# Turning the rank stacks on VectorE in squares of 32, in a kernel of four chained adapter layers

## What is computed

```python
x = x + _L0_cond_ref(...)  # x @ W.T + 2 * gated expert adapters of rank 16, top 2 of 8
x = x + _L1_cond_ref(...)  # W = weights[condition]; einsum('bct,bcd->bdt', x, W)
x = x + _L2_cond_ref(...)  # Bx = einsum('bni,bri->bnr', x, B[ids]); einsum('bnr,bor->bno', Bx, A[ids])
x = x + _L3_cond_ref(...)  # x @ W.T + b + ((x @ A[ids]) @ Bm[ids]) * 2, rank 16
```

## Time and profile before

| | us |
|---|---|
| median of three runs | 906.36 (905.24 to 906.5) |
| the profiled execution | 905.11 |
| its span, first to last instruction | 903.3 |
| TensorE busy | 894.3 |
| VectorE busy | 557.0 |
| ScalarE busy | 346.6 |
| GpSimd busy | 235.9 |

### The profile page before, as it was taken

The page is one execution under the profiler, slowest core; times in us unless marked ns, Lnnn a source line. Parts: engine busy times, 40 slices in busy tenths (PEclk is TensorE's granted clock), DMA queues, the critical chain, the costliest instruction groups (busy, mean ns, idle before and its releaser), DMA issues.

```text
span 903.3 us, 14862 instructions
## 1 busy us (share of the span) xinstructions
PE 894.3 (99%) x4758; PEld 794.6 (88%) x4758; DVE 557.0 (62%) x1421; ACT 346.6 (38%) x800; POOL 235.9 (26%) x379
## 2 busy tenths in 40 slices
PE   8999999999999999999999999999999999999997
PEld 7888888888888888998998998998999999999997
DVE  6554444444367526567667677677676686686675
ACT  5543343333334332333433434424434334334333
POOL 1010010011010003524424425415415325235240
PEclk9999999999999999999999999999999999999999
DMA  7878686999663564666765766666567567667665
GB/s 251 306 249 292 209 255 204 311 337 266 186 193 124 167 197 143 179 181 188 214 183 179 209 198 192 194 199 210 172 202 221 174 181 221 185 183 218 186 197 155
DMA packets 105602, 187.69 MB, mean 208 GB/s; under 512 B 15926, under 2 KB 66870, under 8 KB 105526
## 3 DMA queue, kind: packets, MB, share of 16 engines
q1 hardware_dynamic: 105526, 186.76, 67.6%
HBM read 143.20 MB, written 49.81 MB: 214 GB/s over the span
## 4 chain that ended last, share of the span: by engine, by line
PE 91%; SPq 3%; DMA 2%; issue 1%; POOL 1%; DVE 0%; ACT 0%; DVEq 0%; POOLq 0%
PE ps_o L1407 27%; PE ps_d L1433 17%; PE ps_w L1441 13%; PE ps_d L1441 10%; PE ps_s L1407 8%; PE ps_o L1454 5%; PE ps_d L1448 4%; PE ps_o L1465 2%; DMA mdraw<-t 1%; PE ps_s L1471 1%; SPq L445 1%; PE ps_w L1448 1%; DMA stat_raw<-stat 1%; SPq L403 1%; PE ps_o L1503 0%
## 5 line engine op out<-in xcount | busy, mean ns | idle before, releaser
L1042 DVE TENSOR_TENSOR stat_lo<-stat_raw,stat_hi 128x1024 fp32r<-128x1024 f32 (+1 forms) x127 | 147.5, 1162 | 26.5 <-ACT stat_hi L773 24.2
L773 ACT ACTIVATE stat_hi<-stat_raw 128x1024 fp32r<-128x1024 f32 (+1 forms) x127 | 116.9, 933 | 22.3 <-POOL stat_raw L657 7.5
L1433 PE MATMUL ps_d<-w_hi,stat_hi 128*128 128x512 f32 x256 | 104.9, 410 | 0.7 <-POOL w_lo L682 0.7
L1433 PE MATMUL ps_d<-w_lo,stat_hi 128*128 128x512 f32 x256 | 101.2, 395 | 0.0
L1433 PE MATMUL ps_d<-w_hi,stat_lo 128*128 128x512 f32 x256 | 100.8, 394 | 0.0
L1407 PE MATMUL ps_o<-chunk_a_hi,stat_hi 128*128 128x512 f32 x216 | 84.4, 391 | 0.9 <-DVE stat_lo L1042 0.9
L1407 PE MATMUL ps_o<-chunk_a_hi,stat_lo 128*128 128x512 f32 x216 | 84.1, 389 | 0.0
L1407 PE MATMUL ps_o<-chunk_a_lo,stat_hi 128*128 128x512 f32 x216 | 84.0, 389 | 0.0
L682 POOL CAST w_hi<-mdraw 128x512 fp32r<-128x512 f32 x32 | 19.6, 613 | 206.1 <-DMA mdraw<-t 206.1
L657 POOL TENSOR_TENSOR stat_raw<-stat_raw,ident 128x128 f32<-128x128 f32 x40 | 22.9, 574 | 184.2 <-DMA stat_raw<-stat 184.2
L1407 PE MATMUL ps_o<-chunk_b_hi,stat_hi 128*128 128x512 f32 x152 | 59.1, 389 | 0.0
(11 more groups left out here) (226 smaller groups left out, 2266.7 us busy)
## 6 DMA issues: line engine op xcount, KB each, us to landing
up<-tu SPq DMA_DIRECT2D x124, 256.0 KB, 4.3
stat_raw<-stat SPq DMA_DIRECT2D x59, 512.0 KB, 4.4
mdraw<-t SPq DMA_DIRECT2D x128, 208.0 KB, 2.9
stat_raw<-x SPq DMA_DIRECT2D x32, 512.0 KB, 3.5
out<-outb SPq DMA_DIRECT2D x30, 512.0 KB, 5.3
t<-md_a SPq DMA_DIRECT2D x16, 576.0 KB, 5.8
rows_raw<-x SPq DMA_DIRECT2D x32, 256.0 KB, 3.4
chunk_a_raw<-mov SPq DMA_DIRECT2D x24, 256.0 KB, 5.1
```

What stands on the lines that cost most here:

```text
L773: return nc.scalar.activation(dst, src, ACT.Copy)
L1042: return nc.vector.tensor_tensor(out=dst, in0=src, in1=rounded.bitcast(F32), op=ALU.subtract)
L1433: last = nc.tensor.matmul(plain_bank(t)[:, 0:WCOLS], rows[a][:, k, :], w[c][:, k, :], start=k == 0 and m == 0, stop=k == KB - 1 and m == l ...
```

## The change

The transpositions on TensorE (`h2_rows`, `h3_rows`) go. After each stack VectorE writes the transposed stack to a tile `turned` in SBUF, in eight squares of 32x32 (`turn_ranks`), and ScalarE rounds `turned` into `h2T` or `h3T`. The stacks are 64 columns wide instead of 128, both batch rows in the same columns; the zero blocks are in `turned`, cleared once. There is one `turned`, so a turn waits until the copy of the turn ahead has been made; since `h2T` is now overwritten without a step of TensorE in between, its copy waits until the products of the tile ahead are done. In the last pair some steps of `ranks` are written in another order. The number that a turn has in the order is given by `h2_place` and `h3_place`.

```diff
-        h2stack = sb("h2stack", [P, BT, RANK, 2, 2], F32R)
-        h3stack = sb("h3stack", [P, BT, RANK, 2, 2], F32R)
+        h2stack = sb("h2stack", [P, RANK, 2, 2], F32R)
+        h3stack = sb("h3stack", [P, RANK, 2, 2], F32R)
+        turned = sb("turned", [P, TOKENS])
...
+        def h2_place(turn):
+            return 2 * turn + (0 if at(turn, TURN_A) else 1)
+        def h3_place(turn):
+            return 2 * turn + (3 if at(turn, TURN_B) else 2)
...
             def h2_hi(t):
                 act.wait_ge(pe_h, t + 1)
+                if not at(t, 0):
+                    act.wait_ge(dve_turned, h2_place(t - 1))
...
             def h2T_copy(t):
-                act.wait_ge(pe_h2T, t + 1)
-                round_to(h2T[:, :], ps_h2T).then_inc(act_h2T, 1)
+                act.wait_ge(dve_turned, h2_place(t))
+                if not at(t, 0):
+                    act.wait_ge(pe_up2, t)
+                    act.wait_ge(pe_h3, t)
+                round_to(h2T[:, :], turned[:, :]).then_inc(act_turned, 1)
...
             def h3T_copy(t):
-                act.wait_ge(pe_h3T, t + 1)
-                round_to(h3T[:, :], ps_h3T).then_inc(act_h3T, 1)
+                act.wait_ge(dve_turned, h3_place(t))
+                if not at(t, 0):
+                    act.wait_ge(pe_out[2], t)
+                round_to(h3T[:, :], turned[:, :]).then_inc(act_turned, 1)
...
+            def turn_ranks(stacked, place):
+                flat = stacked[:, :, :, :].rearrange("p r h e -> p (r h e)").bitcast(F32)
+                if place > 1:
+                    dve.wait_ge(act_turned, place - 1)
+                for b in range(BT):
+                    for i in range(b * TB, (b + 1) * TB, SQUARE):
+                        for q in range(0, 4 * RANK, SQUARE):
+                            row = b * 4 * RANK + q
+                            last = nc.vector.transpose(turned[row:row + SQUARE, i:i + SQUARE],
+                                                       flat[i:i + SQUARE, q:q + SQUARE])
+                last.then_inc(dve_turned, 1)
...
                 last.then_inc(dve_h2, 1)
+                dve.wait_ge(dve_h2, t + 1)
+                turn_ranks(h2stack, h2_place(t))
...
             def ranks2(t):
-                pe.wait_ge(act_h2T, t + 1)
+                pe.wait_ge(act_turned, h2_place(t))
...
-                plain(a, range(0, 3))
-                if fin:
-                    h3_rows(b2)
-                plain(a, range(3, 5))
+                plain(a, range(0, 5))
                 if fin:
                     ranks3(b2)
...
                 winograd(ps_w, A11, B11, True).then_inc(pe_p[0], 1)
-                if back:
-                    pe.wait_ge(dve_vsum, 2 * a + 2)
-                    pe.wait_ge(dve_h2, a1 + 1)
-                    h2_rows(a1)
...
-                plain(b, range(0, HALF_KB))
+                plain(b, range(KB)).then_inc(pe_hl, 1)
+                if back:
+                    ranks3(a1)
                 pe.wait_ge(dve_udb, a + 1)
-                if back:
-                    h3_rows(a1)
-                plain(b, range(HALF_KB, KB)).then_inc(pe_hl, 1)
-                if back:
-                    ranks3(a1)
                 gated_rows(a)
```

More of the change, by code:

```diff
@@ L361, in build @@
         pe_out = [sem(f"pe_out{n}") for n in range(3)]
-        CONSTS = 6
+        CONSTS = 5
+        SQUARE = 32
         SETS = BT + 8
@@ L893, in h2_hi @@
                 act.wait_ge(pe_h, t + 1)
+                if not at(t, 0):
+                    act.wait_ge(dve_turned, h2_place(t - 1))
                 for b in range(BT):
                     rows = slice(b * TB, (b + 1) * TB)
-                    last = round_to(h2stack[rows, b, :, :, 0], hidden(t, rows, slice(b * RANK, (b + 1) * RANK)))
+                    last = round_to(h2stack[rows, :, :, 0], hidden(t, rows, slice(b * RANK, (b + 1) * RANK)))
                 last.then_inc(act_h2, 1)
@@ L900, in h3_hi @@
                 act.wait_ge(pe_h3, t + 1)
+                if not at(t, 0):
+                    act.wait_ge(dve_turned, h3_place(t - 1))
                 for b in range(BT):
                     rows = slice(b * TB, (b + 1) * TB)
-                    last = nc.scalar.activation(h3stack[rows, b, :, :, 0], hidden(t, rows, slice(BR + b * RANK, BR + (b + 1) * RANK)),
+                    last = nc.scalar.activation(h3stack[rows, :, :, 0], hidden(t, rows, slice(BR + b * RANK, BR + (b + 1) * RANK)),
                                                 ACT.Copy, scale=SCALE3)
@@ L1210, in mix_lo, with stack_lo @@
                 rest(mix[t % 2][lo][:, :], mixid[t % 2][:, :], mix[t % 2][hi][:, :]).then_inc(dve_mix, 1)
-            def stack_lo(t, rows, b, cols, stacked, scale):
+            def stack_lo(t, rows, cols, stacked, scale):
                 src = out_bank(t, 0)[rows, cols][:, :, None].to_broadcast([TB, RANK, 2])
-                return nc.vector.scalar_tensor_tensor(out=stacked[rows, b, :, :, 1], in0=src, scalar=scale,
-                                                      in1=stacked[rows, b, :, :, 0].bitcast(F32), op0=ALU.mult,
+                return nc.vector.scalar_tensor_tensor(out=stacked[rows, :, :, 1], in0=src, scalar=scale,
+                                                      in1=stacked[rows, :, :, 0].bitcast(F32), op0=ALU.mult,
                                                       op1=ALU.subtract)
+            def turn_ranks(stacked, place):
[9 more added lines that the diff above has]
+                last.then_inc(dve_turned, 1)
             def h2_lo(t):
@@ L1221, in h2_lo @@
                 for b in range(BT):
-                    last = stack_lo(t, slice(b * TB, (b + 1) * TB), b, slice(b * RANK, (b + 1) * RANK), h2stack, 1.0)
+                    last = stack_lo(t, slice(b * TB, (b + 1) * TB), slice(b * RANK, (b + 1) * RANK), h2stack, 1.0)
                 last.then_inc(dve_h2, 1)
+                dve.wait_ge(dve_h2, t + 1)
+                turn_ranks(h2stack, h2_place(t))
             def h3_lo(t):
@@ L1227, in h3_lo @@
                 for b in range(BT):
-                    last = stack_lo(t, slice(b * TB, (b + 1) * TB), b, slice(BR + b * RANK, BR + (b + 1) * RANK), h3stack, SCALE3)
+                    last = stack_lo(t, slice(b * TB, (b + 1) * TB), slice(BR + b * RANK, BR + (b + 1) * RANK), h3stack, SCALE3)
                 last.then_inc(dve_h3, 1)
+                dve.wait_ge(dve_h3, t + 1)
+                turn_ranks(h3stack, h3_place(t))
             def hidden_sum(t):
@@ L1565, in fore @@
                     pe.wait_ge(dve_Ra_raw, j)
-                plain(b, range(0, HALF_KB))
-                pe.wait_ge(dve_udb, a + 1)
-                if back:
-                    h3_rows(a1)
-                plain(b, range(HALF_KB, KB)).then_inc(pe_hl, 1)
+                plain(b, range(KB)).then_inc(pe_hl, 1)
                 if back:
                     ranks3(a1)
+                pe.wait_ge(dve_udb, a + 1)
                 gated_rows(a)
@@ L1648, in last @@
                 mixed_piece(TURN_B, b, 0).then_inc(pe_h, 1)
-                pe.wait_ge(dve_udb, b + 1)
-                h3_rows(b1)
                 pe.wait_ge(dve_Rb_part, j + 1)
```

40 lines of the change are left out of this document (13 added, 27 removed).

## The result

| | before | after |
|---|---|---|
| median, us | 906.17 (905.24 to 907.92, 6 runs) | 932.38 (931.23 to 934.99, 6 runs) |
| span of the profiled execution, us | 903.3 | 930.5 |
| ratio | | 1.0295, 95% interval 1.0283 to 1.0306 |

The change makes the kernel slower by 26.2 us. The forecast was slower by 14.2, at 920.6 us, with a range up to 932.0: the direction and the first place were right, the size was not, and the time lies just outside the range.

What follows compares the result with a forecast made beforehand. TensorE was taken as the bound, with no idle time left. Terms -6.4 + 13.1 + 3.4 + 4.1 = +14.2 us on the 906.4 median gave 920.6 us, range 904 to 932.

Steps and rivals of the forecast that it cites:

- The saving: On TensorE, 58 of the 64 removed transpositions give back 0.11 us each, 6.4 us.
- The squares: On VectorE, eight squares per stack, 0.20 us each without overlap, take 1.6 us together.
- The rivals with overlap: VectorE's squares overlap: fully, 903.6 us, chance 0.13; half of them overlapping or short squares, 909.5 us, chance 0.12.
- h2 of the even tile: TensorE waits at the first product with h2T, 15 times, for ScalarE's copy behind the exponential; 13.1 us.
- T - 0.81: TensorE's wait at the even tile's h2T in 13 pairs: eight squares' time less 0.81, 0.79 us each.
- the stretch: Sign against the forecast: it would be wrong if squares stretch while GpSimd works.
- h3 of the odd tile: TensorE waits at ranks3, 14 times 0.24 us, since the copy stands behind Ra_hi on ScalarE; 3.4 us.
- T - 1.36: TensorE's wait at the odd tile's ranks3: eight squares' time less 1.36, 0.24 us each.
- The last pair: At the kernel's end six turns bring 9.8 us; even filling all 5.7 us of VectorE's idle time, they add 4.1.
- The rest of the pair: Odd tile's h2, even tile's h3 and removed waits cost nothing; VectorE's lateness, 0 to 0.3 us a pair, counted 0.
- beyond 922: Rival with longer squares: 0.22 us each gives 926.2 us; chance 0.17, of which 0.05 beyond 932.
- thin covers: S rows, hgT and vparts have little slack against late VectorE; 0.3 x 15 takes the longer-squares rival to 930.7 us.

Runs made afterwards that it cites:

- copyboth: Changed kernel with ScalarE's copies to h2T (even tile) and h3T (odd tile) moved ahead of the gate's exponential and of Ra_hi; 928.32 us, 1.0234 of before.
- tail1: Changed kernel with one square in place of eight for each of the last six turns; 926.87 us, 1.0230 of the kernel before.
- k12: Changed kernel with four more squares ahead of each stack's eight, written to a tile nobody reads; 971.98 us, 1.0723 of the kernel before.
- narrow_w: Changed kernel with GpSimd's copies into w cut to one block of eight after the first tile; 927.02 us, 1.0222 of the kernel before.
- odd_vec: Odd tiles' stacks turned on VectorE, even tiles' and the last six on TensorE, h3T copy ahead of Ra_hi; 907.90 us, 1.0020 of the kernel before.

## Why the prediction was right and wrong

- **The saving, -6.4: right.** `copyboth` has 12.449 us from odd to even product and the kernel before 12.671. The difference is 0.222, two transpositions at 0.11. The record's 0.276 would have given 0.55.
- **The squares, T = 1.6: nearly right.** 0.202 us each, in order, T = 1.72, since one starts about 0.015 after the last ends. That makes the sum 4.2 larger: waits at `h2T` 14.9 in place of 13.1, at `h3T` 5.0 in place of 3.4, the end 4.9 in place of 4.1. The rivals with overlap are out. The rule of the Trainium skill (VectorE: DVE Perf Modes, Two Vector instructions with no wait between them), that a changed start quadrant of the output holds an instruction, agrees with the 0.217 from start to start.
- **The steps that failed: three terms of the sum that were too small.** The places were right and the sizes were not. The table sets each term against what the starts of TensorE's products give (the distance to the product ahead, less the 0.165 or 0.23 us that it is without a wait):

| term, us | forecast | its rule with T = 1.72 | measured |
|---|---|---|---|
| 58 transpositions | -6.4 | -6.4 | -6.4 (58 x 0.11, as in `copyboth`) |
| waits at `h2T`, 15 | 13.1 | 14.9 | 15.9 (16.3, and 0.4 before), and 1.4 for the restarts |
| waits at `h3T`, 14 | 3.4 | 5.0 | 6.0, and 1.5 for the restarts |
| the end | 4.1 | 4.9 | 7.7 |
| sum | 14.2 | 18.4 | 26.1 of the 27.2 between the profiles |

- **h2 of the even tile: right place, 13.1 too small.** What the rule T - 0.81 lacked is the stretch of `vparts` beside GpSimd's casts (2.7 us over all pairs) and the restart: behind each wait the next product follows at 0.26 us in place of 0.16. Some was given back, since ScalarE's `u2s` now starts 0.11 us behind the exponential's start, where in the pair of the earlier trace rows it was 0.67, with a wait for a DMA. I had named the stretch as something that would prove me wrong, and priced it at nothing.
- **h3 of the odd tile: right place, 3.4 too small.** The wait is 0.30 us in most pairs (T - 1.36 gives 0.36). One of 1.9 us at 556 us, in a pair where the h3 stack itself is late, and the restarts, 0.11 each, were not in the sum.
- **The last pair, +4.1: mis-sized.** It measured 7.7 in the profiles (5.5 by the medians of `tail1`). The step "even if they fill every gap, the end moves by 4.1" took the case in which all gaps fill for the dearest one. It is the cheapest: six turns filled only 1.9 of the 5.7 us.
- **"The rest of the pair", counted 0: a wrong step that this kernel hides.** I wrote that h3 of the even tile has 2.3 us between copy and product and loses T of it. That holds for the product. It says nothing of what stands on VectorE behind that turn, and there the free part of T is 0.93 us, where the turn brings 1.72. In the changed kernel little of it shows: -0.08 against -0.22 in that half, of which 0.10 are the restart at `h2T`. The wait at `h2T` makes TensorE later against the stack (s is 2.42, it was 2.94), and so covers the lateness. The two prices are alternatives: remove the first and the second is paid, 1.47 us a pair. With k12 both are paid.
- **What is left.** 1.1 of the 27.2 us isn't in the table; 0.8 of it lies ahead of the first product with `h2T`.
- **The chances.** 0.17 stood on "beyond 922" with longer squares and thin covers, at up to 930.7, and 0.05 of it on beyond 932. T came out near that rival's 1.76, by the gaps between squares and not by longer ones, and gives 4.2 of the 12 us that were missing. The other 8 came from the restarts, the stretch, the end and one late pair, which no rival had. That the time lies so near the range's upper end is luck.

What isn't settled: what the short casts of `narrow_w` save ahead of the second pair, and the 4.6 us by which `odd_vec` missed. That an h3 stack moved back to its old place would cost `copyboth` 0.85 us a pair less (3.79 - 2.94) follows from the sum above, and was not tried. The sum was found in the profiles afterwards; only its T was varied by experiment.

## What to carry to other kernels

Before work is moved to an engine that is idle for 30% of the time, add up its idle time in the run of instructions from each insertion to the results that the bound engine waits for, and what these results have to spare; here 0.93 us were free for 1.72, while the pair had 10.0 free. Then ask whether the change moves the start of that run as well. A wait on the bound engine hides lateness behind it, so a repair of the wait that shows is worth no more than the difference to the next one: test it with the suspect removed (one square in place of eight) before you believe its price. At the end of this kernel only 1.9 of the helper's 5.7 us of idle time were cover, since whoever it waits for is late with it.

## What the runs showed of the hardware

- A 32x32 fp32 transposition on VectorE takes 199 to 210 ns in 512 instances, also beside GpSimd's casts. `vparts` (64x32, both inputs in SBUF) takes 184 to 618 ns, and the long ones lie beside a 128x512 cast. The Trainium skill (GPSIMD Engine Reference, Specifications) names contention for VectorE's instructions with two SBUF inputs; the trace agrees: the squares have one input. It is not the whole account: `gsel`, with one tensor and two columns of scalars, takes 278 to 860 ns in the same trace.
- A wait of TensorE costs about 0.1 us more than its length: the product behind it is followed at 0.26 us in place of 0.16 (601.83, 602.09). It stands behind all 15 waits at `h2T`. Of the five waits in `copyboth`'s half of a pair from even to odd product, three show it.
- The granted clock fell where TensorE had been waiting near the end. Windows of the changed kernel, with the clock third from the right:

```profile
922.00:924.00 2.00, 0.83 (x4) 0.46 (x3) 1.87 (x10) 0.07 (x1) 0.00 (x0) 0.99 0.00 0
924.00:926.10 2.10, 1.22 (x3) 0.76 (x3) 2.06 (x7) 0.31 (x1) 0.00 (x0) 0.50 0.15 55
```

```profile
924.79 1.22 PE L1500 MATMUL ps_o<-up,h3T 128*128 128x312 f32 x3 [1.64 <-ACT h3T L782]
```

  0.50 is the lower level, 1.2 GHz. The last three products took 1.22 us there. In the kernel before the same three took 0.74, at full clock:

```profile
897.85 0.74 PE L1465 MATMUL ps_o<-up,h3T 128*128 128x312 f32 x3
```

  So 0.5 us of the end's price is this. TensorE had been busy for 0.83 of the two us ahead.
